# A 3x3 convolution on group-normalized images: the last loads split by partitions instead of by columns

## What is computed

```python
g = x.reshape(8, 16, 2, 128, 128)                      # 16 groups of 2 channels
n = (g - mean(g)) / sqrt(var(g) + 1e-5)                # per image and group
conv = crop(ifft2(einsum(fft2(pad(n, 256)), fft2(pad(weight, 256)))), 64, 64 + 128)
out = x + conv + bias
```

## Time and profile before

| | |
|---|---|
| median of 3 runs | 82.92 us (82.86 to 83.15) |
| profiled execution | 82.75 us |
| its span | 81.5 us |
| TensorE matmul busy | 67.7 us, 83% of the span |
| VectorE, ScalarE, GpSimd busy | 50.2, 48.0 and 31.6 us |
| DMA queue of SyncE | 33.36 MB, 96.1% of 16 engines |
| mean rate of the DMA engines | 412 GB/s |
| mean granted clock of TensorE | 0.954 |

### The profile page before, as it was taken

The page is one execution under the profiler, slowest core; times in us unless marked ns, Lnnn a source line. Parts: engine busy times, 40 slices in busy tenths (PEclk is TensorE's granted clock), DMA queues, the critical chain, the costliest instruction groups (busy, mean ns, idle before and its releaser), DMA issues.

```text
span 81.5 us, 684 instructions
## 1 busy us (share of the span) xinstructions
PE 67.7 (83%) x222; PEld 41.8 (51%) x222; DVE 50.2 (62%) x43; ACT 48.0 (59%) x53; POOL 31.6 (39%) x43
## 2 busy tenths in 40 slices
PE   0019865999999999999999999999999999999000
PEld 0014424556666666666666666666666665665000
DVE  0019936960399779949994996899499735100700
ACT  3308958980299669947974994799299553000000
POOL 6994000004029950000999690086029206800000
PEclk9999995557999999999999999999999999999998
DMA  1999999999979997799597997979969999988976
GB/s 21 336 434 438 458 426 408 457 461 466 482 338 466 399 608 336 336 608 399 238 546 337 490 490 279 529 305 514 498 289 466 418 402 466 480 382 382 525 325 253
DMA packets 2020, 33.62 MB, mean 412 GB/s; under 512 B 280, under 2 KB 314, under 8 KB 484
## 3 DMA queue, kind: packets, MB, share of 16 engines
q1 hardware_dynamic: 1876, 33.36, 96.1%
q0 software_dynamic: 96, 0.19, 0.7%
q10 hardware_dynamic: 48, 0.06, 0.3%
HBM read 16.84 MB, written 16.78 MB: 412 GB/s over the span
## 4 chain that ended last, share of the span: by engine, by line
PE 77%; DMA 14%; DVE 2%; SPq 1%; issue 0%; POOL 0%; POOLq 0%
PE ps L437 75%; DMA images<-x_dram 14%; DVE images L453 2%; PE ps_m L339 1%; SPq L195 1%; PE ps_w L285 1%; POOL pair L233 0%; POOL eps L199 0%; POOLq L605 0%
## 5 line engine op out<-in xcount | busy, mean ns | idle before, releaser
L437 PE MATMUL ps<-g,w_sb 128*128 128x363 f32 (+1 forms) x192 | 61.9, 480 | 0.0
L437 PEld LDWEIGHTS ps<-g,w_sb 128*128 128x128 f32 x192 | 36.6, 197 | 20.5 <-issue 2.3
L418 POOL TENSOR_SCALAR images<-images,bias_sb 128x1984 f32<-128x1984 f32 (+3 forms) x12 | 23.2, 1941 | 26.9 <-ACT origin L313 18.4
L303 DVE TENSOR_REDUCE sums<-images 128x1 f32<-128x4096 f32 x7 | 30.9, 4411 | 0.6 <-DMA images<-x_dram 0.6
L324 ACT ACTIVATE unused<-images,origin 128x4096 f32<-128x4096 f32 (+1 forms) x9 | 30.0, 3331 | 0.3
L453 DVE SCALAR_TENSOR_TENSOR images<-ps,bias_sb,images 128x1089 f32<-128x1089 f32 (+2 forms) x9 | 10.9, 1221 | 7.7 <-PE ps L437 7.7
L394 ACT ACTIVATE g<-images,rstd 128x1089 f32<-128x1089 f32 (+2 forms) x8 | 9.4, 1192 | 3.4 <-DVE rstd L368 3.4
L303 DVE TENSOR_REDUCE first_sums<-images 128x1 f32<-128x2048 f32 x2 | 4.6, 2286 | 5.9 <-DMA images<-x_dram 5.9
L356 DVE TENSOR_SCALAR var<-ps_m,square 128x1 f32<-128x1 f32 x8 | 1.7, 218 | 9.4 <-ACT square L351 9.4
L351 ACT ACTIVATE square<-ps_m,origin 128x1 f32<-128x1 f32 x8 | 2.1, 262 | 8.4 <-PE ps_m L339 8.4
L285 PE MATMUL ps_w<-images,avg 128*128 128x1 f32 x4 | 1.1, 355 | 6.9 <-POOL bias_sb L499 5.9
(11 more groups left out here) (21 smaller groups left out, 13.0 us busy)
## 6 DMA issues: line engine op xcount, KB each, us to landing
images<-x_dram SPq DMA_DIRECT2D x1, 5344.0 KB, 36.8
images<-x_dram SPq DMA_DIRECT2D x1, 4096.0 KB, 24.6
out_dram<-images SPq DMA_DIRECT2D x1, 4096.0 KB
out_dram<-images SPq DMA_DIRECT2D x2, 2048.0 KB
out_dram<-images SPq DMA_DIRECT2D x1, 3904.0 KB
out_dram<-images SPq DMA_DIRECT2D x1, 3040.0 KB
images<-x_dram SPq DMA_DIRECT2D x1, 2080.0 KB, 15.5
images<-x_dram SPq DMA_DIRECT2D x2, 1024.0 KB, 5.8
```

The source lines that it names most:

```text
L303: lambda e: e.tensor_reduce(to_sum(img, k)[:, 0:1], piece, mybir.AxisListType.X, ALU.add),
L418: "pool", lambda e: e.tensor_scalar(part, part, 1.0, bias_sb, op0=ALU.mult, op1=ALU.add),
L437: lambda e, k=k, dc=dc, rows=rows, top=top: e.matmul(ps[:, 0:rows, 0 : N - dc], w_sb[:, k * P : (k + 1) * P], g[:, top : top + rows, dc:N] ...
```

## The change

The last two loads no longer split the rest of the columns between them. The first of them now brings partitions 0 to 111 and the second partitions 112 to 127, each with all that is left of the row (12,224 numbers, 48,896 bytes). So every image from 5 on, but for the first row of image 5, now needs both. `loaded` is written accordingly: the entry `(0, begin)` makes every operation on images 6 and 7 wait for both loads. In `take_std` the shift of image 4 gets a wait for the second load, so that what follows on VectorE and ScalarE has seen it. The store of images 0 and 1 still waits for `begin`, which is now the load of 112 partitions.

```diff
-    LAST = 24
+    FIRST = 112
...
-    begin = load_rows(5 * H + 1, B * H - LAST)
-    loaded[5] = [(1, third), (H, begin)]
-    loaded[7] = [(H, begin)]
-    loaded[6] = [(H - LAST, begin), (H, load_rows(B * H - LAST, B * H))]
+    rest = slice((5 * H + 1) * W, B * H * W)
+    begin = load(whole[0:FIRST, rest], source[0:FIRST, rest])
+    tail = load(whole[FIRST:P, rest], source[FIRST:P, rest])
+    loaded[5] = [(1, third), (1, begin), (H, tail)]
+    loaded[6] = loaded[7] = [(0, begin), (H, tail)]
...
         first_ok[img] = put(
             "pool", lambda e: e.tensor_copy(sums[(img - 1) % 2][:, 2:3], xts[img][:, 0, 0:1]),
-            *rows_in(img, H if img == B - 2 else 1), *needs, *([group_ok[img - 3]] if img > 3 else []), mark=True,
+            *rows_in(img, 1), *needs, *([group_ok[img - 3]] if img > 3 else []), mark=True,
         )
...
             lambda e: e.tensor_scalar(
                 rstds[img][:, 1:2], ps_ms[:, 0:1], rstds[img][:, 0:1], -1.0, op0=ALU.mult, op1=ALU.mult
             ),
-            rstd_ok, mark=True,
+            rstd_ok, *([tail] if img == 4 else []), mark=True,
         )
```

## The result

The changed kernel takes 97.83 us (97.52 to 98.54, 6 runs) against 82.93 us in runs beside it: 1.181 times as long, with an interval of 1.176 to 1.186. Its span is 96.5 us, 15.0 more than before. The direction was forecast, the size was not, and the time lies above the range.

A forecast was written before the change was run, and what follows sets the result against it. TensorE and the DMA engines were taken to bound the kernel side by side. Landing 0.9 + 5.0 us later moves the span from 81.5 to 87.4; plus 1.25 and 0.17, 88.8 us. Own range 85.5 to 91.5, widened to 82.6 to 91.5.

The forecast's parts named there:

- What bounds the kernel: Whole kernel: two bounds side by side, TensorE up to 77 us and the DMA engines over the whole span.
- The load of 112 partitions: First of the two last loads: lands 0 to 1.8 us later than its predecessor; the middle, 0.9 us, taken.
- Its high end: 112-partition load: 48,896 bytes per partition at 3.33 GB/s, 14.7 us, so 1.8 us later.
- The load of 16 partitions: Second of the two last loads: 6.9 us instead of 1.9, so 5.0 us more; the deciding term.
- the pace taken from the weights' load: 16-partition load: 7.07 GB/s per partition, from the narrow weights' load to 32 partitions, gives 113 GB/s.
- The sum: Last landing moves from 42.4 by 0.9 + 5.0 to 48.3 us; span ends at 87.4, time 88.8 us.
- The upper end of the range: Forecast's own range up to 91.5 us: 1.8 us for the first load and 8.7 for the narrow one.
- The far end that was left out: Narrow load at 3.33 GB/s per partition, 14.7 us, would give 97.5 us; left out with less than 0.1.
- The added wait, TensorE's clock: Ahead of image 4's shift: TensorE stalls 3.8 us, then 14 products at the 1.2 GHz level lose 3.0 us.
- no change: Rival on the 16-partition load: pace is the engine's, last landing stays at 42.4 us; 82.9 us, chance 0.25.
- The two loads beside each other: Rival: the 16 fill engines the 112 leave half filled, both land at 42.3 us; 84.2 us, chance 0.08.
- The 1.3 us for an empty stretch: In the rival of both loads beside each other: nothing left to move while SyncE issues the first store, 1.3 us.

The follow-up runs named there:

- the single load: Changed kernel with one load of all 128 partitions, same rows of 48,896 bytes, in place of the two: 84.72 us, 1.022 times the kernel before.
- the order of eight loads: Kernel before, last 768 KB load cut into eight loads of 16 neighbours (85.55 us); then only their order changed, each second load 32 partitions below: 87.12 us.

## Why the prediction was wrong

*What bounds the kernel*: right. TensorE's row and the DMA stream moved by 15.3 and 15.0 us, next to nothing was made up later, and the stores after the last landing took 38.8 us as against 39.1.

*The load of 112 partitions*: this term failed. It was given 0.9 us, between 0 and 1.8, and cost 11.9. Its high end said that "a partition takes no more than it takes now", 3.33 GB/s; it took 225 / 112 = 2.01. The ends were drawn from two paces, that of an engine and that of a partition, as if one of them had to hold. What counted in these runs is which partitions make up a load, and in which order the loads come: a row took 3.4 us in the load of 112 and 1.8 in the one of 128. That engines collide where they write at the same moment fits all of them; which engine writes which partition no view shows. I treated 112 as nearly 128; the run with one load of 128 shows the jump between them.

*The load of 16 partitions*: right in kind, too large in its place. It was given 6.9 us, 5.0 more than before, and took 5.3 beyond the first, 3.4 more. Of whole rows to 16 neighbours, the pace taken from the weights' load, 113 GB/s, was met (109 to 111). The difference is overlap: its 16 rows started between 48.7 and 51.7 us, before the other load landed at 52.4, and took 6.0 us each in the mean.

*The sum*: the landing came 9.4 us later than forecast. 11.9 + 3.4 stand where 0.9 + 5.0 stood. The upper end of the range (1.8 and 8.7) stretched the wrong term. The far end that was left out, 97.5, lies near the 97.83 by luck: it gave 12.8 us to the narrow load and 1.8 to the wide one, and these cost 3.4 and 11.9.

*The added wait, TensorE's clock*: right in kind. The wait was met late and held TensorE for 14.6 us against 3.8 forecast: 9.4 of the difference are the later landing, and 1.35 that TensorE came to image 4 earlier in this execution. The clock fell to the 1.2 GHz level, and cost 2.1 us (6.29 against 4.2) instead of 3.0.

*The rivals*: "no change" fell with the landing at 57.7. The two loads beside each other did not come either: the rows of the 16 began only at 48.7 us, and they landed 5.3 us after the 112. The 1.3 us for an empty stretch before the first store was a fair size: the single load showed 1.2 to 1.8.

## What to carry to other kernels

Cut a load by columns, not by partitions: the 128-partition transfers here ran at 410 to 440 GB/s, and every cut of these whole rows into two loads about halved it, whether at 64, 96 or 112. Where partitions must be cut, look at which of them are written at the same time; loads of 16 partitions apart moved 193 GB/s and of 16 neighbours 110, with the DMA engines busy for over 0.9 in both, so read that share beside GB/s. For a term that no row shows, don't draw both ends from the two nearest paces without asking whether a third thing can be the limit.

## What the runs showed of the hardware that was not expected

A load of 112 of 128 partitions takes about twice as long as one of all 128 with as many bytes (24.5 us against 12.7, counted from the landing of the 4096 KB load near 28). The pace within it is not even, by busy time of the changed kernel:

```profile
30.00:33.60 3.60, 3.60 (x12) 1.92 (x11) 3.60 (x2) 2.95 (x2) 0.00 (x0) 1.00 0.95 217
33.60:37.00 3.40, 2.98 (x13) 2.03 (x12) 2.23 (x5) 1.78 (x4) 0.00 (x0) 1.00 1.03 230
37.00:39.60 2.60, 2.60 (x10) 1.64 (x9) 2.60 (x1) 2.57 (x3) 2.30 (x1) 1.00 0.99 301
39.60:42.20 2.60, 2.60 (x11) 1.73 (x10) 1.85 (x3) 1.64 (x3) 2.60 (x2) 1.00 1.02 301
```

By the port map of the Trainium skill (SBUF — State Buffer, section "Door 1: The DMA port swizzle"), and if each engine writes seven partitions in a row (an assumption that no view here proves), two pairs of engines share a port in the first three rows, one pair in the fourth and the fifth, and two pairs again in the sixth and the seventh. 217 to 230 and then 301 GB/s fit that order, and so do the packets: a row took 3.2 to 3.5 us in the first three steps, 2.6 in the next two, 3.2 and 3.5 in the last two (means).

But with two pairs of 16 engines sharing, 12 should go at full pace. In the second step all 16 rows took 3.39 to 3.56 us, and none the 1.8 of the single load. Why all are slowed alike was seen and is not explained.

The other surprise is that the order of eight loads, with nothing else changed, moved the time from 85.55 to 87.12 us.
